# A graph network kernel in which the matmuls that fetch the rows of Q are issued twice

## The reference, cut to what matters

```python
src, dst = node2edge_index[0], node2edge_index[1]
messages = jnp.concatenate([node_rep[src], edge_rep[dst]], axis=-1)
messages = _bn_relu(messages @ W1, g1, b1)          # statistics over all 50000 edges
edge_new = segment_sum(messages, dst, ...)
aggregate = segment_sum(edge_new[dst], src, ...)
```

## Time and profile before

| what | us |
|---|---|
| median of 3 timed runs | 3788.69 (3786.29 to 3794.76) |
| profiled execution, its own time | 3754.2 |
| its span | 3752.5 |
| PE busy in the span | 2420.2 |
| DVE busy | 2253.4 |
| POOL busy | 1744.7 |
| ACT busy | 1348.1 |
| mean share of TensorE's full clock | 0.758 |

### The profile page before, as it was taken

The page is one execution under the profiler, slowest core; times in us unless marked ns, Lnnn a source line. Parts: engine busy times, 40 slices in busy tenths (PEclk is TensorE's granted clock), DMA queues, the critical chain, the costliest instruction groups (busy, mean ns, idle before and its releaser), DMA issues. The chain is left out here.

```text
span 3752.5 us, 38369 instructions
## 1 busy us (share of the span) xinstructions
PE 2420.2 (64%) x11894; PEld 1975.0 (53%) x11894; DVE 2253.4 (60%) x4208; ACT 1348.1 (36%) x2765; POOL 1744.7 (46%) x1293
## 2 busy tenths in 40 slices
PE   5787544444444357750004998607999999973998
PEld 4422244444444345540004884406889888962688
DVE  6899677777777788860003442403564564535788
ACT  4488444434444200000002333303434434433676
POOL 0258877667667676767776767770000000024000
PEclk8888755555555568885557999758999999975999
DMA  9992355656556766651115661116546545512255
GB/s 350 355 322 26 49 169 170 169 168 173 167 164 172 161 158 184 187 124 0 0 0 122 177 156 1 1 0 171 171 132 187 173 132 171 162 53 53 84 174 177
DMA packets 339434, 521.99 MB, mean 139 GB/s; under 512 B 144970, under 2 KB 226691, under 8 KB 332195
## 3 DMA queue, kind: packets, MB, share of 16 engines
q1 hardware_dynamic: 197144, 446.27, 36.8%
q0 software_dynamic: 135920, 61.61, 14.2%
q10 hardware_dynamic: 6170, 11.66, 1.0%
HBM read 370.82 MB, written 148.58 MB: 138 GB/s over the span
## 5 line engine op out<-in xcount | busy, mean ns | idle before, releaser
L1054 PE MATMUL banks<-rows_r,lhs_r 128*128 128x448 f32 x3500 | 897.9, 371 | 517.4 <-issue 358.3
L1054 PEld LDWEIGHTS banks<-rows_r,lhs_r 128*128 128x128 f32 x3500 | 664.7, 190 | 588.6 <-issue 507.5
L669 POOL DMA_INDIRECT counts<-wts x391 | 615.2, 1573 | 378.2 <-issue 202.7
L678 POOL DMA_INDIRECT weights<-wts x391 | 634.0, 1621 | 253.5 <-issue 247.6
L498 DVE SCALAR_TENSOR_TENSOR ring_r<-ring,dinv,rows_r 128x896 fp32r<-128x896 f32 (+1 forms) x300 | 303.3, 1033 | 440.7 <-ACT rows_r L486 440.6
L686 POOL DMA_INDIRECT reg<-tab_p,w x440 | 426.1, 968 | 230.2 <-issue 120.5
L1054 PE MATMUL banks<-ring_r,lhs_r 128*128 128x448 f32 x1750 | 525.1, 370 | 0.0
L486 ACT ACTIVATE rows_r<-ring,dinv 128x896 fp32r<-128x896 f32 (+1 forms) x300 | 284.9, 951 | 515.0 <-PE banks L1054 345.1
L496 DVE TENSOR_TENSOR ring_r<-ring,rows_r 128x896 fp32r<-128x896 f32 x200 | 191.9, 973 | 445.1 <-ACT rows_r L484 444.8
L732 POOL DMA_INDIRECT el<-tab_l,base_i x25 | 24.0, 959 | 810.3 <-DMA tab_l<-reg 803.0
L484 ACT ACTIVATE rows_r<-ring 128x896 fp32r<-128x896 f32 x200 | 170.6, 857 | 510.2 <-DMA ring<-counts 358.9
(11 more groups left out here) (250 smaller groups left out, 3842.2 us busy)
## 6 DMA issues: line engine op xcount, KB each, us to landing
ring<-weights SPq DMA_DIRECT2D x225, 448.0 KB, 3.3
ring<-counts SPq DMA_DIRECT2D x150, 448.0 KB, 3.3
zbuf<-reg SPq DMA_DIRECT2D x220, 256.0 KB, 3.0
reg<-zbuf SPq DMA_DIRECT2D x55, 1024.0 KB, 4.7
counts<-ring SPq DMA_DIRECT2D x25, 1568.0 KB, 15.8
weights<-ring SPq DMA_DIRECT2D x25, 1568.0 KB, 17.6
ring<-cells SPq DMA_DIRECT2D x38, 448.0 KB, 4.3
ring<-weights SPq DMA_DIRECT2D x75, 224.0 KB, 3.2
```

The lines of the kernel that those rows point to most:

```text
L669: pool.indirect_dma_start(counts, bass.IndirectOffsetOnAxis(ap=ix_c[:, k:k + 1], axis=0), vals_c[:, k:k + 1], None, compute_op=ALU.add).th ...
L678: pool.indirect_dma_start(weights, bass.IndirectOffsetOnAxis(ap=ix_w[:, k:k + 1], axis=0), vals_w[:, k:k + 1], None, compute_op=ALU.add).t ...
L1054: m = pe.matmul(bank[:, 0:BLK], lhs[part], rows[:, c:c + BLK], start=first, stop=last)
```

## The change

In `add_q` the loop over the two chunks of a pair runs over them twice:

```diff
-                for k in (2 * q, 2 * q + 1):
+                for k in (2 * q, 2 * q + 1, 2 * q, 2 * q + 1):
                     for part in (q_high, q_lo):
                         m = pe.matmul(ps[4 + q % 2][:, k % 2 * H:(k % 2 + 1) * H], oT[q // 4 % 2][:, k % 8 * P:(k % 8 + 1) * P],
                                       part[:, bass.ds(tiles[q], 1), :], start=part is q_high, stop=part is q_lo)
                 m.then_inc(zq_done, 1)
```

## The result

The changed kernel takes 3927.43 us in the median of 4 runs (3923.44 to 3937.47), the kernel before, timed beside it, 3791.73 (4 runs, 3786.29 to 3800.76). The ratio is 1.0359, with a 95% interval of 1.033 to 1.0389: slower by 136 us, where I had forecast 80 with a range up to 129. The sign and the place are right, the size is not. The profiled execution of the changed kernel took 3923.4 us. The one of before shown above took 3754.2, 34 to 38 us less than the timed runs of the same kernel; that difference turns out to be part of the answer.

What follows compares the result with a forecast made beforehand. POOL's DMA stream was taken to set the end, with PE and DVE pacing it in the loop; 0.75 x 66 + 0.25 x 121 = 80 on 3788.7 gave 3869 us, range 3830 to 3918.

Steps and rivals of the forecast that it cites:

- What sets the end: Whole kernel: POOL's stream of indirect DMAs has nothing to skip, so a microsecond POOL loses in the loop is lost in total.
- 0.86 us per pair at 1.2 GHz: PE in the loop: four added matmuls at 0.215 us lengthen each pair, its step going from 1.72 to 2.57 us.
- the quarter without a rise: Loop passes: one in four was taken to stay at 1.2 GHz, entering the sum as 0.25 x 121.
- the faster rival: First pair and degrees of a pass: clock rises early or stays up between passes, some -25 us, 3764; chance 0.05.
- +43 for a rise at 4.7 us: Loop: the clock rises 4.7 us into each burst; group passes 0.86 us longer, plain ones 0.9; sum 43.
- +66 for one at 7: Loop: the clock rises 7 us into the burst; group passes 1.2 us longer, plain ones 1.8; sum 66.
- the mix: Loop: rise at about 7 us in three passes of four, none in the fourth; 0.75 x 66 + 0.25 x 121 = 80.
- 1.5 of a pair in the first and last passes: Top of the range: no rise, with the first and last passes at 1.5 of a pair, given as 3918.
- the 3.27 us of DVE's idle time: DVE ahead of a pass's first addition: said to stand idle 3.27 us in both plain and group passes.
- these 34.5 us: Total time: the timed runs' median lies 34.5 above the profiled execution, so 80 was added to 3788.7, giving 3869.
- it costs more: Loop: repeated group starts at a larger distance than 0.215, or gathers and additions fall out of step; 3928; chance 0.06.
- some 190: Sign in the loop: POOL's wait for L1487 up from 110 to some 190, by as much as the whole.

Runs made afterwards that it cites:

- before_again: The kernel before, unchanged, run and profiled once more, on chip 10; measured 3788.41 us.

## Why the prediction was wrong

**What sets the end.** Right in the main. POOL's stream carries the loss, and the last gather and the last weights are later by nearly the same amount (165, then 157 us; 56, then 49 on chip 6). Some 7 to 9 us are made up between the two, so not every microsecond is carried.

**0.86 us per pair at 1.2 GHz.** Right: 2.58 from pair to pair, the first addition 2.28 behind PE's first.

**The clock.** In the passes 2 to 49 of both profiles no burst goes without 2.4 GHz. The rise comes 3.4 to 8.9 us behind its start, in 61 of 86 bursts 4.0 to 6.5, so the quarter without a rise, 0.25 x 121 = 30 of my 80, does not exist. I had also left out of the sum that PE may enter the group pass behind a plain pass at 2.4 GHz: it does so in all 14, and on chip 6 it keeps this clock through the burst in 10 of them. That was the mechanism of the faster rival, and it cuts these passes to +0.44 us each, though it wins nothing. The Trainium skill ("TensorE: Matmul & The Clock Gate", "What's actually happening") has the activity of PE release the clock. In this loop the added matmuls did, where before 7.00 of 7.00 busy us left it at 0.50.

**The size of the terms.** Where there is no hold-up the change costs 20 x 1.73 (GG) + 14 x 1.00 (P) + 14 x 0.44 (PG) = 55 us, which the timed runs confirm with +55. Forecast were +43 for a rise at 4.7 us, +66 for one at 7, and +80 for the mix. The mechanism was right and the mix too dear by 25. Two smaller slips of the prediction change nothing in this: 1.5 of a pair in the first and last passes puts the top of the range at 3912 and not 3918, and the 3.27 us of DVE's idle time stand ahead of the plain pass alone, where the group pass behind it has 0.2.

**The step that failed** is the last: "The timed runs have their median 34.5 above that execution, so I forecast 3788.7 + 80 = 3869." I carried these 34.5 us as a constant. They are mostly a cost of their own, in before_again 14 hold-ups of 2.2 us, and it grows with the instructions that are added: each PG pass of the changed kernel takes 5.7 us more than before_again's, where without hold-ups it takes 0.44 more. With the small rest in GG and P that is 134 - 55 = 79 of its 136 us, a term that I had put at nothing. The two errors point opposite ways, 25 us too much and 79 too little, so that the miss of 56 is smaller than the second alone: that is luck. My rival "it costs more" had 0.06 and another mechanism. No row of the trace shown held this, since the trace was one without hold-ups, with all its records and a time like chip 6's (3754 us, and 3750 there); the 34.5 us between it and the timed runs were the only sign, and I didn't ask what they were. Why completions come late on some chips and not on others stays open.

**What would show it.** GG passes of 20.2 (19.3 to 20.6 forecast) and plain passes of 10.9 to 11.1 (10.7 to 13.2) hold on both chips. POOL's wait for L1487 came to 161 on chip 6 and 266 with hold-ups, for "some 190".

## What to carry to other kernels

When the profiled execution lies outside the spread of the timed runs, find out which passes make the difference before adding a forecast to either; it may be a cost that the change multiplies. Time a change on more than one chip: here the same edit is +55 us or +136, and an edit of SyncE alone 0 or +79. Repeated work between two engines that take turns costs its first part in each turn, and a clock that rises late gives only the rest back.

## What the runs showed of the hardware

- With 16 full matmuls a pass the clock stayed at 1.2 GHz, also with 16 narrow ones beside them (0.50 in the loop of both); with 32 full ones it rose in each burst of the passes 2 to 49, came down again in the pauses of a group, and outlasted PE's pause of 1.3 to 3.2 us behind a plain pass.
- On chips 3, 5 and 10 PE's completions came late in the bursts behind a short pass, and later when instructions were added, on PE or on SyncE alone: the event of `zq_done` came up to 11.2 us behind its matmul instead of 0.43. SyncE's met waits, some 60 ns an instruction without it, were held up too. The traces of such runs lack over a quarter of the semaphore records. None of the six traces of chip 6 shows any of this.
- Degree matmuls of 50 columns as fp32r instead of fp32 took 88 us instead of 182 in the loop, and the kernel became 0.46% to 0.61% faster (-13 and -22 us on two chips), with these operands rounded.
